# Ahead of the loop: the swap first, operand stores split by heads, the second batch's statistics sooner

## The reference, cut to what matters

```python
xn = (inputs - mu) / jnp.sqrt(var + 1e-05) * ln_gamma + ln_beta
xh = xn.reshape(b, s, H, Dh)                      # 8 heads of 16 features
q, k, v = xh @ Wq + bq, xh @ Wk + bk, xh @ Wv + bv
p = pe @ Wp                                       # pe: the positional encoding
content = jnp.einsum('bqhd,bkhd->bhqk', q + u_bias, k)
pos_score = _rel_shift(jnp.einsum('bqhd,khd->bhqk', q + v_bias, p))
attn = jax.nn.softmax((content + pos_score) / jnp.sqrt(jnp.float32(e)), axis=-1)
ctx = jnp.einsum('bhqk,bkhd->bqhd', attn, v).reshape(b, s, e)
x = x + ctx @ Wo + bo
```

## Time and profile before

| | us |
|---|---|
| three runs | 1699.0, 1705.15, 1702.66 (median 1702.66) |
| the profiled execution | 1699.13 |
| its span, from first to last instruction | 1697.4 |
| PE busy | 1549.0 (91% of the span) |
| DVE busy | 1424.4 (84%) |
| POOL busy | 1112.0 (66%) |
| ACT busy | 1085.2 (64%) |
| mean granted TensorE clock | 0.948 |

### The profile page before, as it was taken

How to read it: one execution, slowest core, us unless ns; L and a number is a source line. 1 busy time by engine, 2 the same in 40 slices (tenths; PEclk the granted TensorE clock), 3 DMA queues, 4 the chain that set the end, 5 groups by cost and what they waited for, 6 DMA issues and landing times. The chain is left out here.

```text
span 1697.4 us, 50666 instructions
## 1 busy us (share of the span) xinstructions
PE 1549.0 (91%) x12534; PEld 1209.0 (71%) x12535; DVE 1424.4 (84%) x5423; ACT 1085.2 (64%) x2143; POOL 1112.0 (66%) x2070
## 2 busy tenths in 40 slices
PE   2599999999999999999999999999951699999997
PEld 1366677777677767777776776777641699999997
DVE  3389989999999999999998999999964588888786
ACT  2137677767767767776776776677630577777775
POOL 3337767766776776776676677677663276666666
PEclk8569999999999999999999999999975799999999
DMA  5625543643643553364365345446454244434433
GB/s 162 193 62 151 165 115 100 183 121 103 185 134 100 151 167 110 107 179 128 103 177 140 93 134 165 117 114 171 126 158 125 44 55 55 56 52 55 57 52 49
DMA packets 131860, 199.98 MB, mean 118 GB/s; under 512 B 18392, under 2 KB 93032, under 8 KB 131648
## 3 DMA queue, kind: packets, MB, share of 16 engines
q1 hardware_dynamic: 105792, 177.20, 36.8%
q0 software_dynamic: 25856, 20.27, 8.1%
HBM read 108.24 MB, written 75.33 MB: 108 GB/s over the span
## 5 line engine op out<-in xcount | busy, mean ns | idle before, releaser
L1036 DVE CUSTOM_DVE_ANT_0 junk<-pA,lmask 128x512 bf16<-128x512 f32 x1056 | 694.0, 683 | 79.6 <-PE pA L646 62.2
L947 ACT ACTIVATE prob<-pB 128x512 f32<-128x512 f32 x384 | 229.5, 598 | 196.4 <-PE pB L665 126.3
L1515 POOL DMA_INDIRECT out<-yb,dst x144 | 236.9, 1645 | 129.5 <-ACT yb L1589 74.2
L644 PE MATMUL pA<-K,QL 96*128 96x512 f32 (+3 forms) x792 | 284.9, 361 | 2.0 <-DVE acc L1036 1.3
L667 PE MATMUL pB<-QL,K 97*128 97x512 f32 (+3 forms) x768 | 282.8, 368 | 0.0
L665 PE MATMUL pB<-QU,K 97*128 97x512 f32 (+3 forms) x640 | 265.0, 414 | 1.0
L646 PE MATMUL pA<-K,QU 96*128 96x512 f32 (+3 forms) x660 | 233.4, 355 | 3.3 <-DVE acc L1036 2.3
L949 ACT ACTIVATE prob<-pB 128x512 f32<-128x512 f32 x384 | 227.9, 593 | 13.2 <-PE pB L667 2.2
L683 PE MATMUL pC<-prob,vext 128*17 128x256 f32 x3088 | 215.8, 382 | 0.1
L551 POOL TENSOR_TENSOR prob<-prob,upper_diag 128x128 f32<-128x128 f32 x384 | 194.1, 505 | 32.1
L665 PEld LDWEIGHTS pB<-QU,K 97*128 97x128 f32 x640 | 121.4, 190 | 79.8 <-issue 54.9
(11 more groups left out here) (299 smaller groups left out, 3641.9 us busy)
## 6 DMA issues: line engine op xcount, KB each, us to landing
QL<-split_operands SPq DMA_DIRECT2D x67, 256.0 KB
QU<-split_operands SPq DMA_DIRECT2D x67, 256.0 KB
K<-split_operands SPq DMA_DIRECT2D x67, 256.0 KB
xg<-routed_rows SPq DMA_DIRECT2D x76, 132.0 KB
split_operands<-c_h SPq DMA_DIRECT2D x18, 512.0 KB
split_operands<-c_l SPq DMA_DIRECT2D x18, 512.0 KB
QL<-split_operands SPq DMA_DIRECT2D x67, 128.0 KB
QU<-split_operands SPq DMA_DIRECT2D x67, 128.0 KB
```

The source lines that it names most:

```text
L644: mm = pe.matmul(dst[:, 0:low], QL[0:KROWS, s, q], K[0:KROWS, s, k0:k0 + low], start=True, stop=True)
L947: act.activation(p[:, 0:HALF], pB[:, 0:HALF], ACT.Exp, scale=SCALE).then_inc(p_exp, 1)
L1036: v.tensor_tensor_reduce(out, src[:, :], lmask[:, at:at + HALF], 1.0, -3.0e38, ALU.add, ALU.max, acc[:, s, qb, n % 2:n % 2 + 1]).then_inc( ...
L1515: po.indirect_dma_start(dram["out"], bass.IndirectOffsetOnAxis(dst[k][:, a:a + 1], 0), yb[k][:, a, :], None, compute_op=ALU.add).then_inc( ...
```

## The change

- SP: the second batch's `xt` is loaded and the swap issued ahead of every store.
- SP: the stores of the first batch's parts are cut in two by heads (`store_half`): heads 0 to 3 lie in partitions 0 to 63, heads 4 to 7 in the others. The halves with heads 0 to 3 go first, the stacks of heads 0 to 2 wait for these alone, and after them follow the load of `xres` (which stood ahead of the swap) and the halves with heads 4 to 7.
- SP: the stores of `pe` for the second half of the DRAM tensor go behind `maximum_row(0)`, ahead of the three small loads; two waits for all these stores stand ahead of the loop.
- POOL: `residual(0)` goes behind `rstd(1)` and the router's constants.
- DVE: the statistics of the second batch go between the fourth and the fifth `low`.
- PE's and ACT's instructions stay as they are.

```diff
@@ -233,7 +233,7 @@
-        EVEN, MOVED_N = P - 16, 48
+        EVEN, MOVED_N, HALF_P = P - 16, 48, P // 2
@@ -289,32 +289,46 @@
+            def store_half(nb, op, low, row, name, half, done):
+                sp.dma_start(stored_to(nb, op, low, row)[H // 2 * half:H // 2 * (half + 1)],
+                             parts[name][low][HALF_P * half:HALF_P * (half + 1), :].bitcast(F32)).then_inc(done, 16)
+
+            def store_halves(name, half):
+                for op, row in PLACES[name]:
+                    for low in range(2):
+                        store_half(0, op, low, row, name, half, first_stored)
+
             sp.sem_inc(d_x2, 16)
-            sp.wait_ge(set_dve, DVE_SET)
-            for nb in range(2):
-                for low in range(2):
-                    sp.dma_start(stored_to(nb, 2, low, 1), parts["pe"][low][:, :].bitcast(F32)).then_inc(pe_stored, 16)
             sp.wait_ge(ln, LN_N)
             sp.dma_start(xt[:, :, :], dram["x"][1 % B].rearrange("(t p) e -> p t e", p=P)).then_inc(d_x, 16)
-            sp.dma_start(xres[:, :, :], dram["x"][B - 1].rearrange("(t p) e -> p t e", p=P)).then_inc(d_res, 16)
             swap(0)
+            sp.wait_ge(set_dve, DVE_SET)
+            for low in range(2):
+                store_half(0, 2, low, 1, "pe", 0, pe_stored)
             for name in READY:
                 sp.wait_ge(hi_done, READY[name])
                 sp.wait_ge(low_done, READY[name])
-                for op, row in PLACES[name]:
-                    for low in range(2):
-                        sp.dma_start(stored_to(0, op, low, row), parts[name][low][:, :].bitcast(F32)).then_inc(first_stored, 16)
-            sp.wait_ge(pe_stored, 64)
+                store_halves(name, 0)
+            sp.wait_ge(pe_stored, 32)
             sp.wait_ge(first_stored, ST_N)
             for h in range(3):
                 stack(0, h)
+            sp.dma_start(xres[:, :, :], dram["x"][B - 1].rearrange("(t p) e -> p t e", p=P)).then_inc(d_res, 16)
+            for low in range(2):
+                store_half(0, 2, low, 1, "pe", 1, pe_stored)
+            for name in READY:
+                store_halves(name, 1)
             sp.wait_ge(m_done, M_PRO)
             maximum_row(0)
+            for low in range(2):
+                sp.dma_start(stored_to(1, 2, low, 1), parts["pe"][low][:, :].bitcast(F32)).then_inc(pe_stored, 16)
             sp.dma_start(wr1[:, :], dram["wr1"]).then_inc(d_r, 16)
...
+            sp.wait_ge(pe_stored, 96)
+            sp.wait_ge(first_stored, 2 * ST_N)
             with batches(nc, sp) as b:
@@ -507,9 +521,6 @@
-            po.wait_ge(m_done, 1)
-            for half in range(2):
-                residual(0, half)
             for i in range(RS_N):
                 rstd(1, i)
@@ -527,6 +538,9 @@
+            po.wait_ge(m_done, 1)
+            for half in range(2):
+                residual(0, half)
             with batches(nc, po) as b:
@@ -1243,10 +1257,12 @@
-            for n in range(LOW_N):
+            for n in range(4):
                 low(0, n)
             for t in range(NB + 1):
                 stats(1, t)
+            for n in range(4, LOW_N):
+                low(0, n)
             for t in range(NB):
                 normalize(1, t)
```

## The result

The changed kernel takes 1710.67 us (median of 4 runs, 1710.26 to 1711.94); the kernel before takes 1702.51 (4 runs, 1699.0 to 1705.15). The ratio is 1.0063, with a 95% interval of 1.0046 to 1.0079: 8 to 13 us slower by the interval, 8.2 by the medians. The forecast was 1710.0.

The account below looks back on a forecast made before the run. PE was busy 91%, but the change touches nothing inside the loop, so a later loop start delays the end. 1699.1 + 8.5 = 1707.6, set on the mean of four executions as 1710.0; own range 1705 to 1715, whole range 1699 to 1716.

Parts of the forecast that it names:

- The swap first: Start of kernel: swap lands at 32.5, POOL's rotation comes 7.4 us earlier, last low part at 43.7.
- The engines' chain: Swap, POOL, DVE and values ahead of PE's first product: 15.0 us earlier, alone allowing that product at 60.8.
- The first halves: Twelve half stores ahead of the stacks: four engines, 2.50 us each; first stack 3.8 earlier, first product at 70.9, gaining 4.9.
- The second halves: Twelve halves queued ahead of the row of maxima: 30.0 us; PE's second pass starts 7.1 later, at 112.3.
- The small loads: Router's loads behind two whole stores (5.0 us): landing at 117.6 instead of 107.92, DVE's first loop tile 9.7 later.
- The first steps of the loop: SP enters the loop at about 117.5; its loads are needed at about 132, so the delay is hidden.
- What DVE wins back: At the loop's start: 1.2 to 1.7 of 9.7 us come back where DVE waited for slow PE; net 8.5 taken.
- rival 3: PE's second pass: waiting for DVE keeps the clock at 0.50 longer, some 3 us more, 1713; chance 0.08.
- The sum: Whole kernel: 1699.1 + 8.5 = 1707.6, with the forecast set on the mean of four executions: 1710.0.
- Rival 1: Half stores take half the time, 1.25 us; engines' chain sets the first product, gain of 10.3, to 1691; chance 0.10.
- Rival 2: Half stores on four faster engines, 2.15 us each: 8.4 won back, no change, 1701.5; chance 0.10.

Follow-up runs that it names:

- halves_in_place: Kernel before with its ten stores of c, k, gl and gu cut in two halves by heads at their place; 1723.98 us against 1700.52 (ratio 1.0143).
- pe_stores_last: Changed kernel with the two whole stores of pe behind the three small loads; 1709.63 us, run again 1709.96 beside the changed kernel's 1711.63.
- halves_wide: Changed kernel with a DRAM layout making a half store 64 rows and a stack nine DMAs; 1688.53 us against 1702.29 for the kernel before (ratio 0.9928).
- whole_stores: Changed kernel with the parts stored whole, all 12 ahead of the stacks; 1703.76 us against 1702.29 for the kernel before (ratio 1.0010).
- swap_only: Kernel before with xt and the swap ahead of the four whole stores of pe; 1704.51 us against 1700.52 (ratio 1.0027).

## Why the prediction was right, point by point

- **The swap first.** Expected in POOL's hands at 32.5, it was there at 31.16, since a swap in an empty queue lands 2.4 after its issue and not the 4.3 of the earlier trace rows. POOL's and DVE's steps beside one another then took longer (below), so that only 0.9 of this was left at the last low part: 42.8, expected at 43.7.
- **The engines' chain.** Expected 15.0 sooner; the values came 14.4 sooner, and PE was done with its projections 10.78 ahead of the stack.
- **The first halves.** The step on which all rested: four engines, 2.50 a half. Measured 105 GB/s, which is 2.50, at a share of 0.26, and 2.53 in `halves_in_place`. The rule of the Trainium skill (DMA: Bandwidth & Descriptors, section "Why a DMA increments its semaphore by 16 and not by 1"), of which the kernel before showed only the case of eight for stores, holds for four and, by the new layout, for sixteen. The first stack went at 64.27, expected at 62.7; the first product at 71.85, expected at 70.9. The sum had every half at its full rate, but from 31 to 36 the halves moved only 45 to 94 GB/s, an estimated 1.4 us.
- **The second halves.** PE's second pass was expected at 112.3 and started at 112.93, released by the row.
- **The small loads.** Expected at 117.6, landed at 118.02. The term is right in this trace, but taking it away brought 1.7 us by the medians; so the loss is first of all that of the second halves.
- **The first steps of the loop.** Hidden, as expected: SP enters the loop at 118.08, and PE waits for no DMA between 113 and 150.
- **What DVE wins back.** This step was wrong. I took 1.2 off the 9.7, as DVE would catch up where PE had been slow. PE was slow again: DVE's fifth tile waited 2.27, and the delay grew from 10.1 to 10.5 there and to 11.6 in the loop, where the forecast had 8.5. What happened is the mechanism of rival 3, the clock. PE ran out of free tiles and waited for DVE until 119.20, and 1.00 came at about 125.6, 6.4 us behind that wait, instead of at 118 to 119. The missing 3.1 us are what rival 3 was priced at. I had given it 0.08 and set it apart, though its condition, PE waiting for DVE, follows from the forecast's own times.
- **The sum.** 1710.0 against 1710.67, and that it is so close is in part luck. In the traces the loss is 3 us more than the 8.5 of the sum; on the other side the base, the mean of four executions, was put 2.4 above the profiled one. By the medians the loss is 8.2, and 8.0 with both kernels on one chip. Mechanism, direction and the large terms are shown; the last 3 us are not settled.
- **Rival 1** fell on the number of engines. I had also said that the trace doesn't bear out the rule of the Trainium skill on ports as a limit, since the stacks reach 253. That reading was weak: the stacks go alternately into partitions 0 to 63 and above, and with two thirds of the bytes in the lower 64 the 253 are an estimated 169 there. For stores out of 64 partitions the runs show a limit: at most 216 GB/s with all engines busy. The Trainium skill (SBUF — State Buffer, section "Door 1: The DMA port swizzle") gives 196 GB/s for 64 partitions and 328 for 128 at 1 MiB a transfer, and about 218 and 436 as what these approach; the measured 216 and 418 lie close under the latter. At four engines a half stays at 105, far under this limit.
- **Rival 2**, engines that run faster when fewer are busy, fell too: 26 GB/s an engine with four, eight and sixteen busy. The 16 GB/s of the loads, from which it was taken, were no property of busy engines.

## What to carry to other kernels

Look at the DMA share where one kind of transfer is alone in the queue: a share far below 1 with a full queue says that its shape, not its bytes, sets the time, and then cutting the transfer along its outermost dimension makes it worse (25 us for ten stores here). Change the layout first, so that the outermost dimension of both sides is large (64 and 128 used all engines here, 8 and 4 did not), and only then the order. And before a transfer is put "between" two others, count all that stands in the queue ahead of the next small one that an engine waits for.

## What the runs showed of the hardware that was not expected

- A store out of 64 partitions moved 211 to 216 GB/s with all 16 DMA engines busy, and one out of 128 partitions 417 to 418. With eight engines busy a whole store moved 210, with four a half moved 105: 26 GB/s an engine, in three shapes, and half of that for 64 partitions on sixteen. That it is the partitions that halve the rate, and not the size of 256 KB, is read from these four cases; no run stores 256 KB out of 128 partitions.
- How long PE's granted clock took to reach 1.00 behind the start of the second pass goes with whether PE was interrupted on the way. Without an interruption it took 5.4 to 8.6 us in nine traces (5.9 in the kernel before; 5.4 and 8.6 in the two runs of one and the same kernel, `pe_stores_last`). With a wait for DVE of 0.83 us it took 9.7 (`halves_wide`), with 1.11 and 1.10 it took 12.7 and 12.6 (the changed kernel, twice), with 5.08 it took 16.9 (`whole_stores`). No run changed the interruption alone. In the first pass ahead of it PE was busy 15.19 of 16 us and the clock stayed at 0.50.
- Within the loop the clock went back to 0.50 for 3.4 or 6.8 us behind a wait of PE of only 1.13 to 1.29 us, in up to two batches of eight, and 3 us of time went with 6.8 at 0.50. Two executions of one kernel differ by such steps, so a gain of 3 us can't be read from one pair of traces.
- POOL's rotation and DVE's low parts took longer when they ran at the same time. In `swap_only` POOL's two products of L464 took 3.48 instead of 2.48 us, and in the changed kernel DVE's two steps `k_l` took 3.41 instead of 1.28.
